# Cross-attention on one core: exponentials divided by their sums before the transpose, on GpSimd; the next stage's first layer norms tile by tile, its first transposes in the last slots

## The reference, cut to what matters

```python
q = jnp.einsum('btc,oc->bto', x, Wq) + bq            # 16 heads of 16
att = jnp.einsum('bhtd,bhid->bhti', q, k) * (1.0 / np.sqrt(D))   # i: 64 context rows
att = jax.nn.softmax(att, axis=-1)
y = jnp.einsum('bhti,bhid->bhtd', att, v)
x = _layernorm(x + (y @ Wo.T + bo))
...
x = x + _msa(_layernorm(x, ln1_w, ln1_b), w_qkv, w_proj)
```

## Time and profile before

| | us |
|---|---|
| median of 3 runs | 1586.13 |
| the profiled execution, its time | 1584.35 |
| its span in the profile | 1582.4 |
| stage of the change, first to last instruction | 153.1 to 359.6 |

### The profile page before, as it was taken

The page is one execution under the profiler, slowest core; times in us unless marked ns, Lnnn a source line. Parts: engine busy times, 40 slices in busy tenths (PEclk is TensorE's granted clock), DMA queues, the critical chain, the costliest instruction groups (busy, mean ns, idle before and its releaser), DMA issues. The chain is left out here.

```text
span 1582.4 us, 44773 instructions
## 1 busy us (share of the span) xinstructions
PE 1473.8 (93%) x18524; PEld 1077.7 (68%) x18524; DVE 1141.2 (72%) x1711; ACT 877.6 (55%) x1606; POOL 378.8 (24%) x601
## 2 busy tenths in 40 slices
PE   7997899977899999999999999999999759999997
PEld 4654677654445666666666666666658649999997
DVE  5787698877868889898988989888846643333332
ACT  2223566654447888888888888888884211111111
POOL 4110332223431111111111111111101024444443
PEclk9998899999999999999999999999999769999999
DMA  6000000002331111111111111111106745656562
GB/s 201 1 21 21 1 2 2 2 1 80 130 138 38 40 39 36 42 36 41 38 39 37 39 41 36 42 37 40 40 6 204 233 159 188 215 186 215 188 210 69
DMA packets 80082, 124.10 MB, mean 78 GB/s; under 512 B 22244, under 2 KB 46950, under 8 KB 79879
## 3 DMA queue, kind: packets, MB, share of 16 engines
q1 hardware_dynamic: 74262, 105.87, 22.2%
q0 software_dynamic: 5616, 15.34, 2.6%
HBM read 94.66 MB, written 26.08 MB: 76 GB/s over the span
## 5 line engine op out<-in xcount | busy, mean ns | idle before, releaser
L548 DVE TENSOR_REDUCE sb_m_mx<-banks 128x1 f32<-128x1024 f32 x512 | 603.4, 1219 | 77.7 <-PE banks L307 69.7
L470 ACT ACTIVATE sb_m_pT<-banks 128x512 f32<-128x512 f32 x1024 | 556.3, 594 | 111.6 <-PE banks L336 100.5
L336 PE MATMUL banks<-sb_m_q,sb_m_k 99*32 99x512 bf16 x4096 | 467.9, 380 | 2.3 <-DMA sb_m_q<-sb_m_mx_parts 1.3
L307 PE MATMUL banks<-sb_m_k,sb_m_q 96*32 96x512 bf16 x4096 | 360.5, 379 | 1.5 <-DMA sb_m_k<-k_parts 1.0
L351 PE MATMUL banks<-sb_m_pT,sb_m_v 128*32 128x256 f32 x4096 | 315.1, 378 | 0.7 <-ACT sb_m_pT L470 0.7
L336 PEld LDWEIGHTS banks<-sb_m_q,sb_m_k 99*32 99x32 bf16 x4096 | 177.8, 95 | 82.2 <-ACT sb_m_pT L470 6.1
L351 PEld LDWEIGHTS banks<-sb_m_pT,sb_m_v 128*32 128x32 f32 x4096 | 175.9, 109 | 60.2 <-ACT sb_m_pT L470 1.2
L307 PEld LDWEIGHTS banks<-sb_m_k,sb_m_q 96*32 96x32 bf16 x4096 | 158.2, 96 | 77.4 <-DVE sb_m_mx L548 5.6
L2437 ACT ACTIVATE sb_e_hT<-banks 128x512 f32<-128x512 f32 x78 | 46.6, 597 | 237.6 <-PE banks L2397 237.6
L228 POOL CAST sb_m_mx_parts<-sb_m_mxT 8x128 bf16<-8x128 f32 x64 | 18.2, 284 | 575.6 <-issue 564.0
L2397 PEld LDWEIGHTS banks<-sb_e_xT,w 128*128 128x128 f32 x1248 | 147.9, 195 | 4.3 <-DVE sb_e_xT L2447 2.4
(11 more groups left out here) (243 smaller groups left out, 1894.3 us busy)
## 6 DMA issues: line engine op xcount, KB each, us to landing
w<-in_w SPq DMA_DIRECT2D x47, 1024.0 KB, 5.2
sb_m_q<-q_parts SPq DMA_DIRECT2D x384, 32.0 KB, 1.8
sb_m_k<-k_parts SPq DMA_DIRECT2D x384, 32.0 KB, 1.8
q_parts<-sb_m_parts SPq DMA_DIRECT2D x24, 256.0 KB, 2.4
k_parts<-sb_m_parts SPq DMA_DIRECT2D x24, 256.0 KB, 2.4
X<-in_x SPq DMA_DIRECT2D x4, 1024.0 KB, 10.0
x_rows<-X SPq DMA_DIRECT2D x8, 512.0 KB, 9.2
z_rows<-sb_g_zs SPq DMA_DIRECT2D x8, 512.0 KB, 5.0
```

What stands on the lines that cost most here:

```text
L307: mm = pe.matmul(ps[2 * (k % 2) + h][c:c + 32, :], q_s[0:R, i, k * P + c:k * P + c + 32], k_s[0:R, i, h * 512:(h + 1) * 512], start=True, ...
L336: mm = pe.matmul(ps[rotating(use)][c:c + 32, :], k_s[:, i2, m * P + c:m * P + c + 32], q_s[:, i2, h * 512:(h + 1) * 512], start=True, stop ...
L470: act.activation(pT[:, m, h * 512:(h + 1) * 512], ps[rotating(f"b{m}{h}")][:, :], ACT.Exp).then_inc(exped, 1)
L548: dve.tensor_reduce(mx[:, par % 2, k:k + 1], pz[:, 2 * (k % 2):2 * (k % 2) + 2, :].rearrange("p q n -> p (q n)"), AX.X, ALU.max).then_inc( ...
```

## The change

- The division moves ahead of the transpose. DVE sums each head's exponentials (a 128 x 1024 reduction in SBUF) and takes 16 reciprocals a row; POOL multiplies the 128 x 1024 exponentials by them, each spread over 64 columns (`weigh`). The products with ones, the reciprocal of 128 x 256 and the multiplication from PSUM go. ACT copies `yT` from PSUM instead. `project` goes to the second half of bank 6.
- Slots: 34 in place of 35. PE's order in a slot is score(n), query, products(n-2), turn, project(n-2), turn_weights(n-1). ACT: prT(n-2), query, yT(n-2), norm, turn, close, exp(n), out(n-2). DVE: sums(n-1), shift, maximum(n), subtraction(n), statistics, closes. POOL: power, add_output(n-3), weigh(n-1), add_bias, close_power.
- The closes: one tile's statistics per slot in slots 11 to 26, moments after every fourth, shift in the slot after that, one tile's norm on ACT per slot in slots 16 to 31.
- `power(2)` goes ahead of the second four bias additions, and `shift_of(2)` behind the first subtraction.
- The next stage's first 16 transposes are issued in slot 32 between project(30) and turn_weights(31), their copies on ACT behind out(30).

```diff
-            turn_tiles(0)
             for b in range(B - 1):
...
-            take_tiles(0, 0)
-            take_tiles(0, 1)
...
+            def weigh(n):
+                pool.wait_ge(rec_done, n + 1)
+                alone(pool, spare)
+                pool.tensor_tensor(pr[:, n % 2, :, :], pr[:, n % 2, :, :],
+                                   rec[:, n % 2, :].unsqueeze(2).broadcast_to([P, H, C]), ALU.mult).then_inc(weighed, 1)
...
             for n in range(SLOTS):
                 g, r = n // GT, n % GT
-                if r == 0 and g + 2 < NG:
+                if r == 0 and 0 < g and g + 2 < NG:
                     power(g + 2)
+                if 0 <= n - 3:
+                    add_output(n - 3)
+                if 0 <= n - 1 < NT:
+                    weigh(n - 1)
                 if g + 2 < NG:
                     add_bias((g + 2) * GT + r)
...
             def turn_weights(n):
-                pe.wait_ge(probs, n + 1)
+                pe.wait_ge(weighed, n + 1)
...
             def products(n):
                 pe.wait_ge(probsT_copied, n + 1)
-                need(pe, yT_done, n)
-                for sums in range(2):
...
+                need(pe, out_copied, n)
+                for j in range(HP):
+                    jj = pair(j)
+                    at = 2 * DK * (jj % 4)
+                    mm = pe.matmul(ps[6][at:at + 2 * DK, jj // 4 * P:(jj // 4 + 1) * P], vblk[:, n // TPB, jj, :],
+                                   prT[:, n % 2, j, :], start=True, stop=True, skip_group_check=True)
...
+                if n == NT:
+                    pe.wait_ge(x_done, 4 * GT)
+                    pe.wait_ge(shifted, NT)
+                    for i in range(TPB):
+                        for k in range(KT):
+                            tr = pe.transpose(ps[2 * (i // 4) + k][:, i % 4 * P:(i % 4 + 1) * P],
+                                              xs_c[:, i, k * P:(k + 1) * P], ident[:, :])
+                        if i % 4 == 3:
+                            tr.then_inc(tiles_turned, 1)
                 if 0 <= n - 1 < NT:
                     turn_weights(n - 1)
...
-            def normalise(n):
-                dve.wait_ge(pv, n + 1)
-                dve.reciprocal(rec[:, :], ps[6][:, D:2 * D]).then_inc(rec_done, 1)
...
+            def sums(n):
+                dve.wait_ge(probs, n + 1)
+                need(dve, rec_done, n)
+                dve.tensor_reduce(total[:, :], pr[:, n % 2, :, :], AX.X, ALU.add).then_inc(total_done, 1)
+                dve.wait_ge(total_done, n + 1)
+                need(dve, weighed, n - 1)
+                dve.reciprocal(rec[:, n % 2, :], total[:, :]).then_inc(rec_done, 1)
...
+                c, k = close_stat_of(n)
+                if c is not None:
+                    close_stat(c, k)
+                    if k == GT - 1:
+                        close_moments(c)
+                c, k = close_stat_of(n - GT)
+                if c is not None and k == 0:
+                    close_shift_of(c)
```

More of the change, by code:

```diff
@@ L1368, in take, with close @@
                                    bias=bias_q[:, part:part + 1]).then_inc(piece_copied, 1)
-            def close(c):
+            def close(c, r):
                 part, own = c % 2, c // 2
+                m = part * GT + r
                 act.wait_ge(close_shift, c + 1)
-                for r in range(GT):
-                    m = part * GT + r
-                    act.activation((X, t["xs_c"])[own][:, m, :], X[:, m, :], ACT.Identity, bias=shift_c[:, r:r + 1],
-                                   scale=rstd_c[:, r:r + 1]).then_inc(x_done, 1)
+                act.activation((X, xs_c)[own][:, m, :], X[:, m, :], ACT.Identity, bias=shift_c[:, c % 2, r:r + 1],
+                               scale=rstd_c[:, c % 2, r:r + 1]).then_inc(x_done, 1)
             for m in range(GT):
@@ L1399, in _ @@
                     take(p, ps[7])
+                if 0 <= n - 2:
+                    act.wait_ge(pv, n - 1)
+                    need(act, out_done, n - 3)
+                    act.activation(yT[:, n % 2, :, :], ps[6][:, 0:D].rearrange("p (k n) -> p k n", k=KT),
+                                   ACT.Identity).then_inc(yT_done, 1)
                 if g + 2 < NG:
                     norm((g + 2) * GT + r)
-                if NT - TPB <= n < NT and n % 2 == 1:
-                    close(n % TPB // 2)
+                for p in turns:
+                    take(p, ps[7])
+                c, k = close_stat_of(n - GT - 1)
+                if c is not None:
+                    close(c, k)
                 if n < NT:
@@ L1407, in _ @@
                                    scale=float(DK) ** -0.5).then_inc(probs, 1)
+                if 0 <= n - 2:
+                    act.wait_ge(out_done, n - 1)
+                    need(act, res_done, n - 3)
+                    act.activation(out[:, n % 2, :], ps[6][:, D:2 * D], ACT.Identity).then_inc(out_copied, 1)
+                if n == NT:
+                    act.wait_ge(t["qkv_in"], 48)
+                    for half in range(2):
+                        act.wait_ge(tiles_turned, half + 1)
+                        for k in range(KT):
+                            act.activation(xT_c[:, k, half * 512:(half + 1) * 512], ps[2 * half + k][:, :], ACT.Identity,
+                                           bias=ln_b[:, k:k + 1], scale=ln_w[:, k:k + 1])
         @block.vector
@@ L1435, in close_shift_of, with close_moments @@
+            def close_moments(c):
+                dve.wait_ge(close_steps, (GT + 1) * c + GT)
+                alone(dve, spare)
+                for r in range(GT):
+                    last = dve.bn_aggr(mv_c[:, r, :], stats_c[:, r, :])
+                last.then_inc(close_steps, 1)
+                dve.wait_ge(close_steps, (GT + 1) * (c + 1))
+                dve.tensor_scalar(mv_c[:, :, 1], mv_c[:, :, 1], EPS, None, ALU.add).then_inc(close_var, 1)
             def close_shift_of(c):
                 dve.wait_ge(close_rstd, c + 1)
-                dve.scalar_tensor_tensor(out=shift_c[:, :], in0=mv_c[:, :, 0], scalar=-1.0, in1=rstd_c[:, :],
+                dve.scalar_tensor_tensor(out=shift_c[:, c % 2, :], in0=mv_c[:, :, 0], scalar=-1.0, in1=rstd_c[:, c % 2, :],
@@ L1460, in _ @@
                 g, r = n // GT, n % GT
-                if 0 <= n - 2 < NT:
-                    normalise(n - 2)
-                if r == 0 and g + 2 < NG:
+                if 0 <= n - 1 < NT:
+                    sums(n - 1)
+                if r == 0 and 0 < g and g + 2 < NG:
                     shift_of(g + 2)
@@ L1472, in _ @@
                                       mx[:, n % 2, :].unsqueeze(2).broadcast_to([P, H, C]), ALU.subtract).then_inc(shifted, 1)
+                if n == 0:
+                    shift_of(2)
                 if g + 3 < NG:
```

133 lines of the change are left out of this document (57 added, 76 removed).

## The result

| | before | after |
|---|---|---|
| median, us | 1587.49 (1585.42 to 1589.29, 4 runs) | 1573.31 (1571.84 to 1576.55, 4 runs) |
| profiled execution, time / span | 1584.35 / 1582.4 | 1576.55 / 1574.6 |
| first layer norm of the stage (ACT) to the barrier behind it | 202.5 | 188.7 |

The changed kernel takes 0.9918 of the time before (95% interval 0.9896 to 0.9940): 14.2 us less, where 8.6 were forecast. The median lies within the range.

What follows compares the result with a forecast made beforehand. The slot was taken as a loop through PE with DVE close behind. Exp(0) at 169.7 + 31 x 5.30 + closes 4.3 + tail 12.7 = 351.0 against 359.6, 8.6 less: 1577.5 us, range 1567 to 1592.

Steps and rivals of the forecast that it cites:

- PE's loop: Project, score, transposes, query, products' first half and the wait for yT on PE: 5.24 us a slot.
- DVE's loop: Maximum, subtraction, ACT's exponential, sum and reciprocal within one slot: 5.20 us a slot.
- Prices: Instruction times worked out from old rows: reciprocal of 128x16 0.25 us, copy to yT 0.39, weigh 2.35 (2.14 to 4.3).
- The POOL loops: Two-slot loops through weigh: 9.85 and 10.15 us at weigh 2.35; POOL sets the slot from weigh 2.6 on.
- Coupling: Steady slots: three loops would not mesh perfectly, adding 0.06 us to the longest, for a slot of 5.30.
- Closes: Spread statistics, shifts, powers and norms in slots 11 to 31 would add 4.3 us: 0.8 + 1.65 + 1.2 + 0.65.
- Start: Stage's beginning: with the third shift no longer ahead of the first maximum, exp(0) at 169.7 us instead of 172.09.
- Tail: From exp(31) to the stage's last addition: 12.7 us against 9.2 before, about 2 of it from the moved transposes.
- POOL as the bound: Spread operand makes weigh dear, so turn_weights and the next score wait: 1600 us at weigh 4.3; chance 0.14.
- Small instructions caught behind weigh: DVE shifts each blocked up to 2.35 us by POOL's weigh; five caught add 11.8 us, giving 1589; chance 0.06.
- No shorter slot: Loops interlock badly and leave the slot at 5.5 to 5.6 us: 1584 to 1587, no change; chance 0.14.
- Better than forecast: Slot of 5.15 us, closes hidden, 2.7 gained in the next stage: 1566 at most, 1571 more probable; chance 0.13.

Runs made afterwards that it cites:

- the first experiment: The changed kernel with the next stage's first 16 transposes and 4 copies taken out of slot 32, back to that stage's start: 1571.63 us, 0.9891 of before.

## Why the prediction was right, point by point

- **What bounds.** "The longest loop of dependences" was right in mechanism and number. PE's loop was put at 5.24, and scores are 5.24 apart; the wait for yT was put at 0.5 and is 0.52. DVE's loop was put at 5.20 and is 5.04: in the last four slots, where PE has no query and no turn, the exponentials stand 5.04 apart, and DVE waits for nothing but the exponential. Over the stage DVE waits for it 0.64 us a slot on the average (20.5 us for 32), just under the 0.7 to 1.1 named.
- **Prices.** Reciprocal of 128x16 0.25 as worked out, sum 1.22, copy to yT 0.38. `weigh` was taken at 2.35 with a lower bound of 2.14, and was 1.90, below the bound. What was wrong is the choice of rows: those in rows 6 read two different wide tiles, and that is what they pay for. The POOL loops as the prediction worked them out, 7.5 or 7.8 + w for two slots, stay under 2 x 5.24 at either price, so the slot should not have changed; the lower price gave 0.45 us more slack. (At w = 2.35 that slack was 0.25 to 0.3 us for two slots by the prediction's own threshold of 2.6, not the 0.5 that it states.)
- **Coupling.** 0.06 us a slot for loops that don't mesh, 1.9 us in all, was not needed.
- **Closes.** The mis-sized term: 4.3 us forecast, 0.3 measured (162.74 less 31 x 5.24). This 0.3 is a net figure: one interval is 5.94 in place of 5.45, which is the closes' 0.5, the first two take 1.0 more than two steady ones, and the last five, without queries, 1.0 less. Its three sub-terms were three shifts waiting 0.55 each for POOL (0, 0.31, 0.68 and 1.04 in the four closes, and hidden in the slack of DVE's loop), statistics beyond the shadow, and powers that push weigh back by 0.6, which with w = 1.90 find slack. Forecast 31 x 5.30 + 4.3 = 168.6, measured 162.7: 5.9 of the difference, and nearly all of it. The misses of coupling and closes point the same way, so the sum was not saved by errors that cancel.
- **Start.** Forecast 2.4 to exp(0), measured 14.66 - 12.81 = 1.85. Score(0) came 0.7 us later behind the first norm than in before, at the lower clock shown with the result, and the shift behind the subtraction met POOL's additions (0.36 us in place of 0.15).
- **Tail.** 12.7 forecast, 12.86 measured. That the moved transposes cost about 2 us there (2.4 by the first experiment) and bring nothing in the next stage was right.
- **Sum.** -1.85 - 15.6 + 3.7 = -13.8, where the prediction had -2.4 - 9.8 + 3.5 = -8.7.
- **Rivals.** POOL as the bound: its loop exists as described (3.80 us give 14 us more than before), its price did not. Small instructions caught behind weigh: not in after, where the shift at 255.90 took 0.15 with weigh starting at 256.16, but shown in full where a second shift was put behind the first. That it loses was said to be improbable for this order, and was. No shorter slot: refuted. Better than forecast: half came true, by the closes; 1573.31 lies at the lower edge of the 1573 to 1582 that the forecast claimed for itself, nearer to this rival's probable 1571 than to 1577.5.
- **Not seen by the prediction.** That the gain depends on two parts together. It priced the spread closes as a cost and said of the blocks of before only that they were there. The experiments show that this is where most of the gain hangs: with blocks the new division is worth 0.5 to 2.4 us, with spread closes 7.6 to 7.7. The rows with blocks show the wait: the new order puts the exponential and its sum into the same slot of DVE, and DVE stands still for 3.09 us while ACT is at the norms.

## What to carry to other kernels

Work out each loop of dependences from measured rows, engine by engine and once along each engine's own order; the longest one gave the slot to 0.01 us, while a reorder that filled the visible wait of one engine lengthened the loop of another and cost 9.6 us in all. When a change makes an engine wait within a slot for something that used to be a slot away, spread what stands ahead of it in bunches first: all parts together gave 14 us, the spreading alone 5, everything else alone 2. Place small DVE instructions with two SBUF operands ahead of a wide POOL instruction (0.26 us was enough here) or behind its end, not at its start or beside it.

## What the runs showed of the hardware

- **POOL's price goes by distinct wide operands.** 128x1024 in float32: 2.36 us with two different tiles, 1.89 with one tile read twice, 1.90 with one tile and a spread operand of 16 columns; addition or product alike. The Trainium skill, page "GPSIMD Engine Reference", section "3.1 Elementwise — side-by-side cycle accounting", puts two-input operations at about 2.6 cycles an element and ascribes it to the reading of two inputs through one port. By that figure and the clock of 1.2 GHz on the same page 1024 columns take 2.2 us, an estimate. The 2.36 us agree with that picture; that a second operand which is the same tile or is spread costs less is not on the page.
- **A small DVE instruction can wait out a whole POOL instruction.** A shift of 128x4 took 0.10 to 0.16 us where no wide instruction of POOL's ran at its start, 0.15 to 0.71 beside additions of 0.73, by how much of them was left, 1.10 beside a weigh of 1.90 that had run for 0.81, and 1.94 and 1.93 beside weighs that had just started. The reductions over 1024 columns beside a weigh kept 1.21 and 1.22. The Trainium skill, page "SBUF — State Buffer", section "Who interferes with whom", says just this: a DVE instruction with two SBUF inputs is blocked whole by a GpSimd instruction that reads SBUF, one with a single input isn't, and the order of issue decides. The trace agrees in the block and in its length. In the records the blocked shift started 0.02 us ahead of weigh (249.45 and 249.47), but DVE's instruction ahead of it, the other shift, ended only at 249.54; so a recorded start can lie ahead of the moment that decides, and the end of the instruction ahead is to be looked at too. From 0.26 us ahead (255.90 and 256.16, 292.26 and 292.52) it was safe.
- **The clock can fall in a tail of 12 us.** In the last 6 us of the stage PE is busy 2 to 4 us. The granted clock there was 1.00 in before, in after and in seven of the experiments' profiles, but 0.50 in one and 0.69, 0.70 and 0.84 in three others. At 0.50 the tail was 1.9 us longer. Stretches at 0.50 lay earlier too, of 3.4 us ahead of exp(31) in before (0.95 us lost) and of 6.8 us ahead of the last 6 us with the closes in fours (2.4 us lost). So a tail is to be read with its clock beside it before a difference of 2 us is given to an edit.
